# The last gathers of an MoE layer paced by another engine's counter

## What is computed

```
g = silu(einsum('nd,edf->nef', flat, wg));  u = einsum('nd,edf->nef', flat, wu)
routed = einsum('ne,nef,efd->nd', comb, g * u, wd)        # 64 experts, 4 per token
sg = silu(einsum('nd,sdh->nsh', flat, swg)); su = einsum('nd,sdh->nsh', flat, swu)
shared = einsum('nsh,shd->nd', sg * su, swd)              # 2 shared experts of width 256
out = x + attention(xn) + routed + shared                 # n = 2048 tokens, d = 256
```

## Time and profile before

| | |
|---|---|
| three runs, median | 406.61 us (401.96, 406.61, 411.38) |
| profiled execution, span | 407.3 us |
| busy in the span | PE 354.1, POOL 257.5, DVE 248.5, ACT 189.3 us |
| the 64 fetches (line 1593) | 61.4 us busy, mean 959 ns |
| the shared experts' units (line 589) | 57.7 us, 128 instructions |
| the shared experts' down products (line 609) | 32.0 us, 128 instructions |
| ScalarE's tanh (line 872) | 9.2 us busy, 66.7 us idle ahead of them |

### The profile page before, as it was taken

The page is one execution under the profiler, slowest core; times in us unless marked ns, Lnnn a source line. Parts: engine busy times, 40 slices in busy tenths (PEclk is TensorE's granted clock), DMA queues, the critical chain, the costliest instruction groups (busy, mean ns, idle before and its releaser), DMA issues.

```text
span 407.3 us, 8670 instructions
## 1 busy us (share of the span) xinstructions
PE 354.1 (87%) x2711; PEld 259.3 (64%) x2711; DVE 248.5 (61%) x717; ACT 189.3 (46%) x359; POOL 257.5 (63%) x522
## 2 busy tenths in 40 slices
PE   6698487988976899899999999999999997989753
PEld 3696355665654556448889999999974544545442
DVE  4668877877876878624554645454444419375676
ACT  3485667686766677533455555555532111010100
POOL 5677986777777665022446566877837757667560
PEclk9969989898999889957999999999999999999969
DMA  8940144444484446545988873577974324434341
GB/s 255 213 109 1 54 131 146 131 146 133 161 241 150 142 146 176 156 141 134 296 263 269 267 249 132 181 244 233 337 252 120 105 85 129 128 94 129 103 129 52
DMA packets 73037, 66.81 MB, mean 164 GB/s; under 512 B 9054, under 2 KB 68702, under 8 KB 72994
## 3 DMA queue, kind: packets, MB, share of 16 engines
q1 hardware_dynamic: 66433, 49.30, 40.8%
q0 software_dynamic: 6144, 16.79, 13.0%
q10 hardware_dynamic: 416, 0.18, 0.2%
HBM read 36.78 MB, written 29.23 MB: 162 GB/s over the span
## 4 chain that ended last, share of the span: by engine, by line
PE 64%; DVE 15%; another core or an unknown queue 8%; issue 5%; ACT 4%; DMA 2%; POOL 1%; SPq 0%; DVEq 0%; ACTq 0%; POOLq 0%
PE bank L650 14%; PE bank L675 8%; PE bank L589 8%; PE bank L515 5%; PE bank L624 4%; PE bank L540 4%; PE bank L609 4%; DVE xall L1092 3%; PE bank L436 3%; PE bank L491 3%; DVE xall L1324 3%; PE bank L417 3%; PE bank L523 2%; PE bank L458 1%
## 5 line engine op out<-in xcount | busy, mean ns | idle before, releaser
L1500 POOL DMA_INDIRECT xs_d<-spare,slot_i x64 | 64.2, 1003 | 29.3 <-PE bank L515 7.5
L1593 POOL DMA_INDIRECT wall<-y_d,y_row x64 | 61.4, 959 | 33.7 <-issue 18.3
L1519 POOL COPY spare<-wall 128x256 f32 x127 | 46.9, 400 | 29.9 <-PE bank L650 18.0
L650 PE MATMUL bank<-xall,spare 128*128 x508 | 64.1, 279 | 0.2
L1284 DVE TENSOR_TENSOR spare<-bank,spare 64x512 f32<-64x512 f32 (+1 forms) x64 | 44.1, 690 | 31.0 <-ACT spare L896 30.1
L650 PEld LDWEIGHTS bank<-xall,spare 128*128 128x128 f32 x508 | 59.4, 192 | 2.8 <-issue 0.7
L589 PE MATMUL bank<-xnT,xall 128*128 128x512 f32 x128 | 57.7, 594 | 0.5 <-issue 0.5
L908 ACT ACTIVATE spare<-bank 128x512 f32<-128x512 f32 (+1 forms) x62 | 33.7, 593 | 29.5 <-PE bank L675 17.9
L847 ACT ACTIVATE xall<-bank 98x1024 bf16<-98x1024 bf16 x32 | 32.7, 1021 | 22.6 <-PE bank L436 14.5
L855 ACT ACTIVATE xall<-bank 128x512 f32<-128x512 f32 x64 | 36.6, 601 | 12.5 <-PE bank L491 7.4
L609 PE MATMUL bank<-xall 128*128 128x256 f32 x128 | 32.0, 400 | 11.6 <-DVE xall L1309 8.3
(11 more groups left out here) (172 smaller groups left out, 656.0 us busy)
## 6 DMA issues: line engine op xcount, KB each, us to landing
y_d<-spare SPq DMA_DIRECT2D x31, 512.0 KB, 4.1
wall<-in_wg SPq DMA_DIRECT2D x16, 256.0 KB, 4.8
wall<-in_wu SPq DMA_DIRECT2D x16, 256.0 KB, 5.0
wdn<-in_wd SPq DMA_DIRECT2D x16, 256.0 KB, 4.5
spare<-xs_d SPq DMA_DIRECT2D x32, 128.0 KB, 2.8
small<-xs_d SPq DMA_DIRECT2D x32, 128.0 KB, 3.3
wall<-in_x SPq DMA_DIRECT2D x4, 512.0 KB, 5.7
base_d<-spare SPq DMA_DIRECT2D x16, 128.0 KB
```

The costliest lines, as they stand in the source:

```text
L650: ins = pe.matmul(up_bank_of(G)[:, j * P:(j + 1) * P], wcur[i % NW][:, c * 2 * F:(c + 1) * 2 * F], x_half[c][:, bass.ds(o, P)], start=c == ...
L1500: pool.indirect_dma_start(out=xs_d, out_offset=bass.IndirectOffsetOnAxis(ap=slot_i[:, T, k:k + 1], axis=0), in_=x_n[b][:, t, :], in_offset ...
L1519: pool.tensor_copy(wcur[i % NW].rearrange("p (c g f) -> p c g f", c=NC, g=2), wall[:, bass.ds(o, WE)].rearrange("p (g c f) -> p c g f", c= ...
L1593: pool.indirect_dma_start(out=yk[:, T, k, :], out_offset=None, in_=of, in_offset=bass.IndirectOffsetOnAxis(ap=y_row[:, T, k:k + 1], axis=0 ...
```

## The change

The wait ahead of a tile's fetches is for VectorE's counter of gated rows in place of TensorE's counter of products, with a number lower by one: tile `T` waits until VectorE has finished unit `T - 1` (`hs >= T`), where it waited until TensorE had finished unit `T`. Everything else, and the order of the instructions on each engine, stays.

```diff
         for T in range(NT):
 
             if T:
-                pool.wait_ge(s["shared"], T + 1)
+                pool.wait_ge(s["hs"], T)
             for k in range(TOPK - 1 if T < FETCH_FIRST else TOPK):
                 fetch(T, k, y_d)
```

## The result

The changed kernel takes 418.38 us (median of 4 runs, 415.04 to 423.82) where the kernel before takes 406.78 us (median of 4, 401.96 to 411.38). The ratio is 1.0327, with a 95% interval of 1.0259 to 1.0394: slower, by 10.5 to 16.0 us. The forecast was 415.5 us, range 402 to 424 us. So I compare stretches within it and not its total.

What follows compares the result with a forecast made beforehand. The prediction took the tail to be bound by TensorE's late marks, released only after POOL stops. Releases 5.0, 6.9 and finally 8.9 us later gave 407.3 + 8.9 = 416.2 us, less 0.7 to the median: 415.5 us, range 402 to 424.

Steps and rivals of the forecast that it cites:

- What bounds the tail: Tail: TensorE's marks reach the counters late, 9.4 us for unit 5, and come some 3 us after POOL stops.
- the jam: Tail: TensorE's marks stuck while POOL issues indirect DMAs without a break, let through some 3 us after POOL stops.
- First stop: Tail: POOL stops at tile 6, not tile 5, for about 5.5 us; unit 5's mark comes 5.0 us later.
- POOL's restart: Tail, after each stop: POOL also waits for ScalarE's tanh and VectorE's two rows, restarting 2.3 us after the release.
- TensorE can't hide it: Tail, first stop: TensorE ran ahead only through unit 7, ending at 335.63 us, so the +5.0 us delays later work.
- the price I had left at nothing: Tail: slow TensorE products behind an idle stretch, up to 2 us if not covered, counted as nothing.
- Second and third stop: Tail: POOL stops at tiles 10 and 14; releases +6.9 us and +8.9 us against the kernel before.
- if its mark is late again, as now: Tail, second stop: unit 9's mark assumed late, holding POOL at tile 10 until release at 364.4 us, +6.9 us.
- 3.2 us from the last fetch to the release: Tail, first stop: late marks come 3.2 us after POOL's last fetch, bounds 2.9 and 3.5.
- Rival B: Tail: POOL's waiting for a TensorE counter while issuing causes the late marks; without it 397.6 us, faster; chance 0.17.
- case D: Tail: only the first stop lengthens, unit 9's mark is punctual; +5.0 us, 411.6 us; likeliest case including it 0.47.
- rival C: Tail: a mark slips through while POOL is busy, so stops lie at tiles 7, 11, 15; +13.9 us, 421 us; chance 0.13.

Runs made afterwards that it cites:

- r3: Kernel before with POOL's wait one higher on TensorE's counter (shared >= T + 2, at most 16), chip with the jam: 399.51 us beside 402.41 us, ratio 0.994.
- m2: Kernel before with wait hs >= T and copies ahead of tiles 6, 10, 14, holding units 5, 9, 13: 417.30 us, ratio 1.034.
- m3: Kernel before with wait shared >= T and copies ahead of tiles 6, 10, 14, holding units 5, 9, 13: 411.29 us, two runs, no ratio.
- m4: Kernel before with stops ahead of tiles 6 and 11 and behind the last fetch, for units 5, 10, 15: 421.56 us, ratio 1.0436.
- r1: Kernel before without any wait ahead of the fetches, on a chip with the jam: 449.38 us beside 404.31 us, ratio 1.1155.
- e1: Kernel before without any wait ahead of the fetches, on a chip without the jam: 372.61 us beside 373.37 us, ratio 0.9985.
- e5: The changed kernel itself against the kernel before, on a second chip, without the jam: 374.08 us beside 373.20 us, ratio 1.0016.
- r2: Kernel before with POOL's wait one higher on TensorE's counter (shared >= T + 2, at most 16), chip without the jam: 374.07 us beside 373.47 us, ratio 1.0023.

## Why the prediction was right, and where it was off

- **What bounds the tail: late marks, ended by POOL's stops.** Right on the chips that have the jam. Without any stop the kernel took 449.4 us where the kernel before took 404.3 on the same chip, and the first release followed POOL's first stop to tile 4 (r3) and to tile 6 (the changed kernel). On the three chips without the jam nothing of it holds, which the prediction did not consider.
- **First stop.** The forecast was tile 6 in place of tile 5, a stop of about 5.5 us, a release 5.0 us later, ScalarE's wait near 19 us. Measured: tile 6, 5.64 us, 4.96 us later (33.16 - 28.20), 18.95 us.
- **POOL's restart 2.3 us behind the release.** 343.31 - 341.00 = 2.31 us. m2 against m3 shows its price apart: 2.6 us more at each later release.
- **TensorE can't hide it.** It lost the time, but not as I told it: unit 7 itself was stretched to 342.9 us, where I had it done at 335.6 and TensorE idle for 6 us after. That its clock fell afterwards was the price I had left at nothing. It does not show in the releases, since TensorE is ahead of POOL's next stop again by then.
- **Second and third stop.** Here the working failed in the profiled execution, in the step "if its mark is late again, as now", by which unit 9 was to hold POOL at tile 10. Unit 9 reached ScalarE at 358.34 us, 1.3 us after its products (353.45 + 3.60 = 357.05 us), so POOL went on to tile 11, and unit 10 was the first one stuck. The second release came 12.85 us later than before and not 6.9, and there was no third stop: POOL's last run of 20 fetches ended the jam by ending. What I had as case D (punctual unit 9, and then only +5 us) began as described and ended the other way: a mark that gets through lets POOL run on, and the next jam is longer. That is the mechanism of rival C, at the second stop. That it came through was chance, as far as these runs show: unit 9's products ended 13.7 us after POOL's restart here (357.05 - 343.31) and 14.9 us after it in the kernel before (349.62 - 334.77), where the mark was stuck, but unit 14's mark, whose products ended 14.0 us after POOL's next restart, came 3.1 us late. The forecast of the whole, +8.9 us, lies under the measured 10.5 to 16.0 (+11.6 by the medians). The two patterns made by hand price this step: m2, with stops at 6, 10 and 14, has the forecast sum (8.9 us in its profile, 10.0 in the medians), and m4, with the pattern seen, is 4.3 us slower. The three other runs of the changed kernel have no profile, so which pattern they had is open; two of them (415.04 and 416.06 us) lie nearer to m2 than to m4. That the forecast of 415.5 us came so close to the median is in part luck: the case in the profile is not the one that it was added up from.
- **3.2 us from the last fetch to the release.** 341.00 - 337.67 = 3.33 and 371.82 - 368.50 = 3.32 us (POOL's restarts less its stops of 5.64 and 5.63 us): within the 2.9 to 3.5 given. It is not a constant, though: 2.8 us after 16 fetches (r3: 323.87 - 321.05), 9.7 after 64 (r1). That is 0.14 to 0.18 us for each fetch of the run. Nor does every mark wait that long: tile 5's came 0.5 us behind the last fetch, 2.8 us ahead of units 10 and 11.
- **Rival B's price.** A tail without a jam takes 86.6 us from the first fetch (e1), where I had worked out 92 (398.3 - 306.3). Against that the tail of the kernel before (101.0 us) loses 14 us. The rest of the 33 us between the chips lies ahead of the tail, where POOL's first fetch comes at 306.33 us against 290.87; the remote waits there are short, and no run shows whether they account for it.

What the jam *is* stays open. It was there on the chip of the result, whose number is not on record, and on three of the six on which the experiments ran, and absent on the other three. Each of the six was used in one sitting, within half an hour altogether (absent, absent, present, present, absent, present), and all runs of a sitting agreed. No chip was tried twice, so that it is the chip and not something that changes with time is likely but not shown. No experiment changed what POOL issues (another kind of DMA, fewer rows), or took the gathers away. The Trainium skill ("Perfetto Trace Analysis", section "DMA Instruction — SWDGE (GPSIMD)") has the profiler's end of such an instruction at the last descriptor written, ahead of the end of the DSP's own code. A backlog that grows with each fetch behind rows of even length would be of that kind; no run here shows what it consists of. Every run here has a span and a granted clock from the profiler, so whether the jam exists without it can't be said either.

## What to carry to other kernels

A wait that protects no data can still set the time: before loosening it, look at what reaches its counter late, and at who gets through only when the waiting engine stands still. When a wait "can't bind" by the rows of the producer but does bind in the profile, the release times belong in a table beside the last instruction of every engine. And an effect found on one chip should be tried on a second before a kernel is tuned around it: here no wait at all is as good as the old one on one chip and 11.6% slower on another (e1 and r1).

## What the runs showed of the hardware

- On some chips TensorE's marks on counters come late while GpSimd issues indirect DMAs back to back: 9.4 us in the kernel before, up to 43.5 us of waiting in r1; on three other chips no wait in the profiles of e1 to e5 and r2 ends in "remote". The same kernel takes 373 us on the ones and 403 to 407 on the others.
- What is stuck arrives some us after the last of the run of DMAs was issued, mostly together: 2.8 to 3.0 us after 16, 3.0 to 3.3 after 20 and 24, 9.7 after 64. Single marks come sooner (0.5 us in the changed kernel) or in the middle of a run.
- In a long jam (from some 27 us into POOL's run in the changed kernel and in r1) TensorE's own products stand apart with gaps of 0.8 to 2.5 us, without any wait that the profile shows, and its granted clock falls (mean 0.63 in the 9 us behind the first jam of the changed kernel, 0.50 from 335 to 378 us in r1, which is the level of 1.2 GHz).
